# A decoder layer on one core: the score weights M stored batch by batch instead of head by head, with filler passes added at the end of TensorE's program

## The chip, the cores and the metric

The kernel runs on one core of a Trainium2 chip. The metric is the device time of one launch in microseconds (us). Every execution reads the same inputs and writes the whole output. Five queues run side by side and meet only at semaphores: PE (TensorE, the matrix engine; its weight loads are listed as PEld), DVE (VectorE), ACT (ScalarE), POOL (GpSimd) and SP (SyncE, which here issues DMAs). SBUF is the working memory that all engines read and write, PSUM the eight banks of 512 words a partition that receive TensorE's results.

## What is computed

x is (16, 256, 128): 16 batches of 256 rows; the context is (16, 64, 128). Three blocks follow one another, each with a residual and a layer norm:

```
x = layernorm(x + attn(x))     # linear attention, 16 heads of 8, elu+1 features, normalised keys
x = layernorm(x + xattn(x, context))
x = layernorm(x + ffn(x))      # fp4-quantised activations and weights, silu(gate) * up, down
# xattn, per head of 64 (16 heads, inner width 1024):
scores = einsum('bhld,bhrd->bhlr', x @ Wq, context @ Wk) * SCALE
out    = einsum('bhlr,bhrd->bhld', softmax(scores), context @ Wv) @ Wo
```

## The kernel before

The work of a batch b is done in T = 2 tiles of 128 rows. The cross attention doesn't build queries and keys. G = Wq Wk^T is made once for each head, and M = G times the transposed context gives, for each batch, a 128 x (16 heads x 64 context rows) matrix, so that the scores of a tile are one product of the transposed row tile with M. To keep the precision of fp32 with single-pass matmuls, both sides are split into a high part and a low part (type fp32r), and three products are summed (PARTS, the pairs high-high, high-low and low-high).

Sizes: HX = 16 heads, R = 64 context rows, BG = 4 batches in a group g, NG = 4 groups, and NQ = 4 quarters q of QH = 4 heads in a group. `m_product(g, q)` (L2768) makes one quarter: 12 matmuls of 256 columns (64 context rows of each of 4 batches) into a pair of PSUM banks, 1,024 words a partition, laid out head, batch, context row. `m_keep_high` (ACT, L975) copies the pair into M as the high part, `m_keep_low` (DVE, L1731) subtracts that from the bank and writes the low part. There are 16 of each over the program, eight of them before 52 us.

`scores(b, t)` (L2841) issues six matmuls of 512 columns: three products for each of two halves of the heads. The moving operand (rhs) is the slice of M of one batch; in the layout before, one head's 64 words stand 256 words from the next head's. `scores_shift` (L2855) then adds the negated row maxima: two matmuls of 512 columns whose moving operand is one word for each head, repeated 64 times.

The order of each engine's program is written out by hand as a list of calls. In PE's list, calls of 16 batches in all stages are interleaved, with `pe.wait_ge` lines between them. `keep_warm(bank, n)` (L2965) issues n matmuls of the identity with itself into a bank that nobody reads at that time. Each is a 128-column fp32 matmul, which the profile shows as two passes. Before, such fillers stand at the very start and at four places at the end of the list. The names in the last stretch: `h_transpose` and `tile_h_transpose` transpose the quantised hidden values `hv` (they wait for POOL's dequantisation, `hq_made`); `down` is the last product of the FFN; `tile_xf_transpose`, `tile_gate_up`, `tile_h_transpose` and `tile_down` do for one tile of batch 15 what the whole-batch functions do for the others; `xfT_kept` counts ACT's copies of the transposed FFN input, `hg4_made` DVE's last rounding of a batch (or tile) of hidden values, `yf_made` DVE's FFN residual. Line numbers in the rows below are those of this kernel.

Of the kernel before, what the change touches and what calls it, by code (L numbers as in the profile page):

```python
# [6 lines left out]
FP32 = mybir.dt.float32  # L7
FP32R = mybir.dt.float32r
INT32 = mybir.dt.int32
ALU = mybir.AluOpType  # L10
ACT = mybir.ActivationFunctionType
AX = mybir.AxisListType

P = 128
# [3 lines left out]
def decoder_layer(nc, x, x_t, attn_w, attn_rows, ctx_t, wq_t, wk_t, wv_t, wo_in, fw_in, out):  # L18
# [9 lines left out]
    R = ctx_t.shape[1] // B  # L28
    HA, DA = 16, 8
    HX, DX = 16, 64  # L30
# [4 lines left out]
    HC = HX // 2  # L35
    BG = 4
    NG = B // BG
    NQ = 4
    QH = HX // NQ
# [22 lines left out]
    with es:  # L62
        def sb(name, shape, dt=FP32):
            return es.enter_context(nc.sbuf_tensor(name, shape, dt))

        def banks(name, n):
            return es.enter_context(nc.psum_tensor(name, [P, n * BANK], FP32))

        def sem(name):
            return es.enter_context(nc.semaphore(name))  # L70
# [24 lines left out]
        ctx_f = sb("ctx_f", [P, B * R])  # L95
        ctx_r = sb("ctx_r", [P, 2, B * R], FP32R)
        HW = sb("HW", [P, 2, NJ, P])
        M = sb("M", [P, 2, 2, HX, BG * R], FP32R)
        w_gu = sb("w_gu", [P, 2, I])
        w_gu_r = sb("w_gu_r", [P, 2, 2, I], FP32R)  # L100
        w_dn = sb("w_dn", [P, NK, P])
# [11 lines left out]
        def several(name, n, shape, dt=FP32):  # L113
            return [sb(f"{name}{k}", shape, dt) for k in range(n)]
# [39 lines left out]
        h = several("h", 2, [P, NH, BLK + 1])  # L154
# [17 lines left out]
        A1, A2, S, TP, F = banks("A1", 1), banks("A2", 1), banks("S", 2), banks("TP", 2), banks("F", 2)  # L172
        F0, F1 = F[:, 0:BANK], F[:, BANK:2 * BANK]
        S0, S1, TP0, TP1 = S[:, 0:BANK], S[:, BANK:2 * BANK], TP[:, 0:BANK], TP[:, BANK:2 * BANK]
# [35 lines left out]
        m_made, m_high, m_low = sem("m_made"), sem("m_high"), sem("m_low")  # L210
# [18 lines left out]
        pT_made, pT_kept, o_made = sem("pT_made"), sem("pT_kept"), sem("o_made")  # L229
# [3 lines left out]
        xfT_made, xfT_kept = sem("xfT_made"), sem("xfT_kept")  # L233
# [4 lines left out]
        ht_made, hg4_made, hq_made = sem("ht_made"), sem("hg4_made"), sem("hq_made")  # L238
        hT_made, hT_kept = sem("hT_made"), sem("hT_kept")
        dn_made, yf_made = sem("dn_made"), sem("yf_made")  # L240
# [13 lines left out]
        def part(w, t):  # L254
            return w[:, t * P:t * P + P]
# [7 lines left out]
        def blocks(ap, n):  # L263
            return ap.rearrange("p (n k) -> p n k", k=BLK)
# [23 lines left out]
        M_BANKS = (TP, S, F, S, F, TP, S, F) + (TP,) * 8  # L288

        def m_bank(g, q):  # L290
            return M_BANKS[NQ * g + q][:, :].rearrange("p (h n) -> p h n", h=QH)

        def m_part(g, q, part):
            return M[:, g % 2, part, QH * q:QH * q + QH, :]

        block = es.enter_context(nc.Block())

# [658 lines left out]
        def _(act):  # L956
            sc = nc.scalar
# [17 lines left out]
            def m_keep_high(g, q):  # L975
                act.wait_ge(m_made, NQ * g + q + 1)
                if g >= 2:
                    act.wait_ge(s_made, T * BG * (g - 1))
                sc.activation(m_part(g, q, 0), m_bank(g, q), ACT.Copy).then_inc(m_high, 1)

            def hw_keep(half):
                act.wait_ge(hw_made, half + 1)
# [192 lines left out]
            k_guess_squared(1, 0)  # L1175
            k_miss_squared(1, 0)
            m_keep_high(0, 0)
            k_exp(2)
            k_guess_squared(1, 1)
            keep_v(2)  # L1180
            k_miss_squared(1, 1)
            m_keep_high(0, 1)
            attn_norm(0, 0)
            m_keep_high(0, 2)
            k_squares(2)
            attn_norm(0, 1)
# [511 lines left out]
        def _(dve):  # L1698
            ve = nc.vector
# [30 lines left out]

            def m_keep_low(g, q):  # L1731
                dve.wait_ge(m_high, NQ * g + q + 1)
                ve.tensor_tensor(m_part(g, q, 1), m_bank(g, q), m_part(g, q, 0).bitcast(FP32), ALU.subtract).then_inc(m_low, 1)

            def x1T_keep_low(b):
                dve.wait_ge(x1T_kept, b + 1)
# [1008 lines left out]
        def _(pe):  # L2745
# [95 lines left out]
            def scores(b, t):  # L2841
                g = b // BG
                pe.wait_ge(x1T_kept, b + 1)
                pe.wait_ge(x1T_low, b + 1)
                if b % BG == 0 and t == 0:
                    pe.wait_ge(m_high, NQ * g + NQ)
                    pe.wait_ge(m_low, NQ * g + NQ)
                for n, (left, right) in enumerate(PARTS):
                    for half in range(2):
                        last = te.matmul(S[:, half * BANK:half * BANK + BANK], part(x1T[b % 2][:, left, :], t),  # L2850
                                         M[:, g % 2, right, HC * half:HC * half + HC, b % BG * R:b % BG * R + R],
                                         start=(n == 0), stop=(n == len(PARTS) - 1))
                last.then_inc(s_made, 1)

# [29 lines left out]
            def xf_transpose(b):  # L2884
                pe.wait_ge(xq_made, b + 1)
                for t in range(T):
                    last = te.transpose(A2[:, t * P:t * P + P], xv[b % 2][:, t * P:t * P + P], ident[:, :])
                last.then_inc(xfT_made, 1)

            def gate_up(b, t):  # L2890
                if b == 0 and t == 0:
                    pe.wait_ge(fwT_kept, 4)
                    pe.wait_ge(gu_high_made, 2)
                    pe.wait_ge(gu_low_made, 2)
                pe.wait_ge(xfT_kept, b + 1)
                if b in WHOLE_GATE:
                    for m, bk in enumerate(ffn_banks(b)):
                        last = te.matmul(bk[:, 0:I], part(xfT[b % 2], t), w_gu[:, m, :], start=True, stop=True)
                    last.then_inc(gu_made, 1)
                    return  # L2900
                pe.wait_ge(xf_low_made, b + 1)
                for n, (left, right) in enumerate(PARTS):
                    for m, bk in enumerate(ffn_banks(b)):
                        last = te.matmul(bk[:, 0:I], part(xf_r[b % 2][:, left, :], t), w_gu_r[:, right, m, :],  # L2904
                                         start=(n == 0), stop=(n == len(PARTS) - 1))
                last.then_inc(gu_made, 1)

            def h_transpose(b):
                pe.wait_ge(hq_made, b + 1)
                for t in range(T):  # L2910
                    for k, k0 in enumerate(KC):
                        c0 = t * BANK + k * P
                        last = te.transpose(TP[:, c0:c0 + P], hv[b % 2][:, t * I + k0:t * I + k0 + P], ident[:, :])  # L2913
                last.then_inc(hT_made, 1)

            def down(b):
                pe.wait_ge(hT_kept, b + 1)
                for t in range(T):
                    if b in SUM_ON_PE:
                        pe.wait_ge(x2_made, T * b + T)  # L2920
                        te.matmul(blocks(part(DN, t), NBX), ident[:, :], x2[b % 3][:, NBX * t:NBX * t + NBX, 0:BLK],
                                  start=True, stop=False)
                    for k in range(NK):
                        last = te.matmul(part(DN, t), hT[b % 2][:, t, k * P:k * P + P], w_dn[:, k, :],  # L2924
                                         start=(k == 0 and b not in SUM_ON_PE), stop=(k == NK - 1))
                last.then_inc(dn_made, 1)
# [10 lines left out]
            def tile_xf_transpose(b, t):  # L2937
                pe.wait_ge(xq_made, b + t + 1)
                te.transpose(part(A2, t), part(xv[b % 2], t), ident[:, :]).then_inc(xfT_made, 1)

            def tile_gate_up(b, t):
                pe.wait_ge(xfT_kept, b + t + 1)
                for m, bk in enumerate(GU_OF[t]):
                    last = te.matmul(bk[:, 0:I], part(xfT[b % 2], t), w_gu[:, m, :], start=True, stop=True)
                last.then_inc(gu_made, 1)
# [19 lines left out]
            def keep_warm(bank, n, w=ident[:, :]):  # L2965

                for _ in range(n):
                    te.matmul(bank[:, 0:P], w, w, start=True, stop=True, skip_group_check=True)
# [549 lines left out]
            pe.wait_ge(yx_made, 15)  # L3518
            xf_transpose(12)
            pe.wait_ge(pT_kept, 30)  # L3520
            h_transpose(11)
            pe.wait_ge(hg4_made, 12)
            gate_up(12, 0)
# [28 lines left out]
            pe.wait_ge(h_made, 29)  # L3552
            gate_up(14, 1)
            pe.wait_ge(hT_kept, 13)
            keep_warm(TP0, 9)
            h_transpose(13)
            pe.wait_ge(yf_made, 13)
            keep_warm(A2, 4)
            tile_xf_transpose(15, 0)
            pe.wait_ge(xfT_kept, 16)  # L3560
            down(13)
            pe.wait_ge(hg4_made, 15)
            tile_gate_up(15, 0)
# [2 lines left out]
            pe.wait_ge(hg4_made, 14)  # L3566
            tile_gate_up(15, 1)
            pe.wait_ge(hT_kept, 14)
            keep_warm(TP0, 7)
            h_transpose(14)  # L3570
            pe.wait_ge(xfT_kept, 17)
            keep_warm(A2, 4)
            down(14)
# [50 lines left out]
```

## Time and profile before

| | us |
|---|---|
| median of 3 runs | 360.56 (360.54 to 360.67) |
| the profiled execution, whole | 362.69 |
| its span, first to last instruction | 360.9 |
| PE busy / DVE busy / POOL busy / ACT busy | 342.2 / 307.8 / 271.8 / 256.0 |
| mean granted TensorE clock | 0.994 |

The profiled execution is 2.1 us longer than the median of the others, and 1.8 us of it lie outside the span. A row of a stretch gives each engine's busy time and, in brackets, how many instructions it had; a row in order of time gives the start, the time from the first start to the last end, and the number of merged instructions. Matmuls are pipelined, so that the duration of one (its mean, or min/median/max) is longer than its distance to the next.

### The profile page before, as it was taken

Reading aid. Unit: us, or ns where it says so; the run is one execution under the profiler, and the core shown is the slowest. Engines: PE = TensorE matmul, PEld = TensorE weight load, DVE = VectorE, ACT = ScalarE, POOL = GpSimd, SP = SyncE. Lnnn points to the kernel's source line nnn. Section 1 sums busy time; section 2 is a strip of 40 time slices with the busy share of each in tenths; the row PEclk is TensorE's granted clock in tenths of the full one; section 3 lists DMA queues with packets and bytes.
Section 4 is the critical chain, followed back from the end, with each engine's and each line's share of the span. In section 5 each row is a group of like instructions: output and inputs, shape, how many; then the busy total and the mean of one; then the engine's idle time right before and its main releaser. Section 6 shows DMA issues by size and latency. Waiting matters only on the chain.

```text
span 360.9 us, 7621 instructions
## 1 busy us (share of the span) xinstructions
PE 342.2 (95%) x2319; PEld 288.1 (80%) x2319; DVE 307.8 (85%) x851; ACT 256.0 (71%) x533; POOL 271.8 (75%) x453
## 2 busy tenths in 40 slices
PE   6789999999999999999999999999999999989884
PEld 6588858787779979977799977888897888968763
DVE  1599986667799998988889988989999987999994
ACT  2678886776788685797857677877877767666543
POOL 3275779889978769798777578979979897794445
PEclk9899999999999999999999999999999999999999
DMA  7821100000100000111001000001000000001001
GB/s 233 290 62 31 39 8 16 0 16 2 46 29 2 1 2 0 45 32 31 0 2 40 7 1 17 15 3 29 2 1 17 1 16 15 4 15 31 0 23 37
DMA packets 13587, 10.46 MB, mean 29 GB/s; under 512 B 971, under 2 KB 12396, under 8 KB 13548
## 3 DMA queue, kind: packets, MB, share of 16 engines
q1 hardware_dynamic: 12540, 7.89, 7.2%
q10 hardware_dynamic: 1008, 2.10, 1.6%
q8 instruction: 19, 0.31, 0.4%
q14 instruction: 20, 0.16, 0.2%
HBM read 7.88 MB, written 2.10 MB: 28 GB/s over the span
## 4 chain that ended last, share of the span: by engine, by line
PE 52%; POOL 16%; issue 14%; DVE 11%; ACT 4%; DMA 1%; POOLq 0%; ACTq 0%; DVEq 0%
PE A L2880 11%; PE S L2850 8%; PE TP L2837 5%; PE TP L2868 5%; PE F L2904 4%; POOL pe L445 3%; PE A L2798 3%; PE A L2924 2%; PE S L2859 2%; POOL fold L439 2%; PE TP L2776 2%; POOL hv L455 2%; DVE smax L1838 2%; PE TP L2913 2%; DMA wqkT<-in_wk_t 1%
## 5 line engine op out<-in xcount | busy, mean ns | idle before, releaser
L445 POOL TENSOR_TENSOR pe<-pe,srec 128x1024 f32<-128x1024 f32 x32 | 60.8, 1905 | 5.0 <-DVE srec L1855 4.9
L2880 PEld LDWEIGHTS A<-wvoT,wqkT 128*128 128x128 f32 x480 | 56.1, 192 | 2.0 <-issue 1.2
L2880 PE MATMUL A<-wvoT,wqkT 128*128 128x128 f32 x480 | 57.3, 275 | 0.0
L2850 PE MATMUL S<-M,x1T 128*128 128x512 f32 x192 | 52.8, 410 | 0.7 <-DVE x1T L1737 0.7
L439 POOL TENSOR_TENSOR fold<-pe 128x512 f32<-128x512 f32 x32 | 42.1, 1314 | 12.6 <-ACT pe L1081 12.4
L2850 PEld LDWEIGHTS S<-M,x1T 128*128 128x128 f32 x192 | 34.0, 189 | 10.4 <-issue 1.8
L1838 DVE TENSOR_REDUCE smax<-S 128x16 fp32r<-128x1024 f32 x32 | 38.9, 1215 | 2.2 <-PE S L2850 2.2
L1086 ACT ACTIVATE wqkT<-TP 128x1024 f32<-128x1024 f32 x32 | 32.7, 1021 | 10.9 <-PE TP L2868 10.8
L1081 ACT ACTIVATE pe<-S 128x1024 f32<-128x1024 f32 x32 | 32.6, 1018 | 5.8 <-PE S L2859 5.6
L2868 PE MATMUL TP<-ident,pe 128*128 128x128 f32 x256 | 33.6, 274 | 0.5 <-ACT wqkT L1086 0.2
L2904 PE MATMUL F<-w_gu_r,xf_r 128*128 128x352 f32 x168 | 33.9, 337 | 0.1
L2868 PEld LDWEIGHTS TP<-ident,pe 128*128 128x128 f32 x256 | 28.8, 140 | 3.7 <-ACT wqkT L1086 0.8
L2837 PE MATMUL TP<-HW,ctx_f 128*64 128x512 f32 x128 | 31.0, 605 | 0.0
L2904 PEld LDWEIGHTS F<-w_gu_r,xf_r 128*128 128x128 f32 x168 | 27.4, 188 | 1.4 <-DVE h L1899 0.5
L1849 DVE TENSOR_REDUCE ssum<-fold 128x16 f32<-128x512 f32 x32 | 21.3, 672 | 6.1 <-POOL fold L439 6.0
L2924 PE MATMUL A<-w_dn,hT 128*128 128x128 f32 x180 | 22.9, 277 | 1.0 <-ACT xfT L1133 1.0
L430 POOL TENSOR_TENSOR kn<-fk,ky 128x256 f32<-128x256 f32 x16 | 11.1, 696 | 16.9 <-DVE ky L1803 16.7
L2924 PEld LDWEIGHTS A<-w_dn,hT 128*128 128x128 f32 x180 | 21.8, 192 | 2.3 <-ACT xfT L1133 1.2
L455 POOL TENSOR_TENSOR hv<-hv,ham 128x704 f32<-128x704 f32 x15 | 20.8, 1388 | 2.5 <-DVE hv L1925 2.4
L2859 PE MATMUL S<-smax,ident_r 128*128 128x512 f32 x64 | 21.4, 416 | 0.7 <-DVE smax L1838 0.7
L423 POOL TENSOR_TENSOR xb<-x_sb,rows 128x512 f32<-128x512 f32 x16 | 20.4, 1279 | 0.5 <-POOL x L488 0.5
L1075 ACT ACTIVATE wvoT<-TP 128x1024 f32<-128x1024 f32 x16 | 16.3, 1021 | 5.7 <-PE TP L2837 5.6
(246 smaller groups left out, 914.6 us busy)
## 6 DMA issues: line engine op xcount, KB each, us to landing
xT<-in_x_t SPq DMA_DIRECT2D x16, 128.0 KB, 2.2
x_sb<-in_x SPq DMA_DIRECT2D x16, 128.0 KB, 2.2
out<-yf SPq DMA_DIRECT2D x15, 128.0 KB, 1.8
pe<-in_fw SPq DMA_DIRECT2D x1, 560.0 KB, 10.6
wqkT<-in_wq_t ACTq DMA_DIRECT2D x2, 256.0 KB, 4.8
wqkT<-in_wk_t ACTq DMA_DIRECT2D x2, 256.0 KB, 6.3
ctx_f<-in_ctx_t ACTq DMA_DIRECT2D x2, 256.0 KB, 7.4
wvoT<-in_wv_t ACTq DMA_DIRECT2D x1, 512.0 KB, 8.9
```

Of the source, the lines that this page charges most:

```text
L439: ge.tensor_tensor(by_head(fold[n % NFO][:, :]), p4[:, :, 0, :], p4[:, :, 1, :], ALU.add).then_inc(fold_made, 1)
L445: ge.tensor_tensor(w, w, spread(srec[n % NFO][:, :], HX, R), ALU.mult).then_inc(pn_made, 1)
L1081: sc.activation(pe_[n % NPE][:, :], S[:, :], ACT.Exp, scale=SCALE).then_inc(pe_made, 1)
L1086: sc.activation(pT[n % 2], TP[:, :].rearrange("p (a n) -> p a n", a=NJ), ACT.Copy).then_inc(pT_kept, 1)
L1838: ve.tensor_reduce(smax[n % 2][:, :], by_head(S[:, :]), AX.X, ALU.max, negate=True).then_inc(smax_made, 1)
L2837: last = te.matmul(TP[par * R:par * R + R, half * BANK:half * BANK + BANK], ctx_f[:, b * R:b * R + R], HW[:, par, 4 * half:4 * half + 4, : ...
L2850: last = te.matmul(S[:, half * BANK:half * BANK + BANK], part(x1T[b % 2][:, left, :], t), M[:, g % 2, right, HC * half:HC * half + HC, b % ...
L2859: last = te.matmul(S[:, half * BANK:half * BANK + BANK], ident_r[:, :], spread(smax[n % 2][:, HC * half:HC * half + HC], HC, R), start=Fal ...
L2868: last = te.transpose(TP[:, j * P:j * P + P], pe_[n % NPE][:, j * P:j * P + P], ident[:, :])
L2880: last = te.matmul(part(A2, t), pT[n % 2][:, j, :], vo[b % 2][:, j, :], start=(j == 0 and b not in SUM_ON_PE), stop=(j == NJ - 1))
L2904: last = te.matmul(bk[:, 0:I], part(xf_r[b % 2][:, left, :], t), w_gu_r[:, right, m, :], start=(n == 0), stop=(n == len(PARTS) - 1))
L2924: last = te.matmul(part(DN, t), hT[b % 2][:, t, k * P:k * P + P], w_dn[:, k, :], start=(k == 0 and b not in SUM_ON_PE), stop=(k == NK - 1))
```

## The change

It has two parts.

1. M's axes are stored as batch, head, context row. `scores` reads 512 words in one run. The two evictions write four runs of 256 words, one for each batch, and read the bank pair as batch, head, context row, that is in 16 pieces of 64 words that stand 256 words apart within one batch. The number of words, of instructions and the order of the calls stay.
2. On PE, fillers are added: 2 ahead of `h_transpose(11)`, a fifth one to the 4 ahead of `tile_xf_transpose(15, 0)`, and 4 ahead of `down(13)`. Some waits stand twice in a row; the second is on a value already reached and merges with the first in the built program.

```
-        M = sb("M", [P, 2, 2, HX, BG * R], FP32R)
+        M = sb("M", [P, 2, 2, BG, HX, R], FP32R)
...
+        def m_by_batch(g, q):
+            return M_BANKS[NQ * g + q][:, :].rearrange("p (h b r) -> p b h r", h=QH, b=BG)
...
         def m_part(g, q, part):
-            return M[:, g % 2, part, QH * q:QH * q + QH, :]
+            return M[:, g % 2, part, :, QH * q:QH * q + QH, :]
...
-                sc.activation(m_part(g, q, 0), m_bank(g, q), ACT.Copy).then_inc(m_high, 1)
+                sc.activation(m_part(g, q, 0), m_by_batch(g, q), ACT.Copy).then_inc(m_high, 1)
...
-                ve.tensor_tensor(m_part(g, q, 1), m_bank(g, q), m_part(g, q, 0).bitcast(FP32), ALU.subtract).then_inc(m_low, 1)
+                ve.tensor_tensor(m_part(g, q, 1), m_by_batch(g, q), m_part(g, q, 0).bitcast(FP32), ALU.subtract).then_inc(m_low, 1)
...
-                                         M[:, g % 2, right, HC * half:HC * half + HC, b % BG * R:b % BG * R + R],
+                                         M[:, g % 2, right, b % BG, HC * half:HC * half + HC, :],
...
             pe.wait_ge(pT_kept, 30)
+            pe.wait_ge(pT_kept, 30)
+            keep_warm(TP0, 2)
             h_transpose(11)
...
             pe.wait_ge(hT_kept, 13)
+            pe.wait_ge(hT_kept, 13)
             keep_warm(TP0, 9)
             h_transpose(13)
             pe.wait_ge(yf_made, 13)
-            keep_warm(A2, 4)
+            pe.wait_ge(yf_made, 13)
+            keep_warm(A2, 5)
             tile_xf_transpose(15, 0)
             pe.wait_ge(xfT_kept, 16)
+            pe.wait_ge(hg4_made, 14)
+            keep_warm(S0, 4)
             down(13)
...
             pe.wait_ge(hT_kept, 14)
+            pe.wait_ge(hT_kept, 14)
             keep_warm(TP0, 7)
             h_transpose(14)
+            pe.wait_ge(xfT_kept, 17)
             pe.wait_ge(xfT_kept, 17)
             keep_warm(A2, 4)
             down(14)
```

PE ahead of `down(13)`, before (L2968 is a filler, L2939 `tile_xf_transpose(15, 0)`, L2924 `down(13)`, L2944 `tile_gate_up(15, 0)`):

```order
L2968 MATMUL A<-ident 128x128 [waits yf_made]
L2968 MATMUL A<-ident 128x128 x3
L2939 MATMUL A<-ident,xv 128x128 [waits xq_made]
L2924 MATMUL A<-w_dn,hT 128x128 [waits hT_kept,xfT_kept]
L2924 MATMUL A<-w_dn,hT 128x128 x5
L2944 MATMUL F<-w_gu,xfT 128x352 [waits xfT_kept,hg4_made]
```

The same place after (L2971 is a filler, L2942 the transpose, L2927 `down(13)`, L2947 `tile_gate_up(15, 0)`):

```order
L2971 MATMUL A<-ident 128x128 [waits yf_made]
L2971 MATMUL A<-ident 128x128 x4
L2942 MATMUL A<-ident,xv 128x128 [waits xq_made]
L2971 MATMUL S<-ident 128x128 [waits hg4_made,xfT_kept]
L2971 MATMUL S<-ident 128x128 x3
L2927 MATMUL A<-w_dn,hT 128x128 [waits hT_kept]
L2927 MATMUL A<-w_dn,hT 128x128 x5
L2947 MATMUL F<-w_gu,xfT 128x352 [waits xfT_kept,hg4_made]
```

What moved: the wait for `xfT_kept` now stands in front of the four new fillers, and `down(13)` follows them.

PE ahead of `h_transpose(11)`, before (L2887 is `xf_transpose(12)`, L2913 `h_transpose(11)`):

```order
L2887 MATMUL A<-ident,xv 128x128
L2913 MATMUL TP<-ident,hv 128x128 [waits hq_made,pT_kept]
L2913 MATMUL TP<-ident,hv 128x128 x5
```

The same place after:

```order
L2890 MATMUL A<-ident,xv 128x128
L2971 MATMUL TP<-ident 128x128 [waits pT_kept]
L2971 MATMUL TP<-ident 128x128
L2916 MATMUL TP<-ident,hv 128x128 [waits hq_made]
L2916 MATMUL TP<-ident,hv 128x128 x5
```

What moved: two fillers start as soon as `pT_kept` allows, and only the transposes behind them wait for `hq_made`.

## Rows read from the trace of the kernel before

**Rows 1.** The page: PE's busy time, and slices of the span with the granted clock

```profile
PE 342.2 (95%) x2319; PEld 288.1 (80%) x2319; DVE 307.8 (85%) x851; ACT 256.0 (71%) x533; POOL 271.8 (75%) x453
...
PEclk9899999999999999999999999999999999999999
```

**Rows 2.** Busy time by stretch: start:end length, engines, granted clock, DMA share, GB/s

```profile
20.00:30.00 10.00, 8.90 (x74) 8.28 (x73) 9.90 (x23) 7.89 (x19) 5.90 (x9) 1.00 0.14 41
...
250.00:300.00 50.00, 50.00 (x343) 41.65 (x342) 47.62 (x132) 36.01 (x71) 45.50 (x75) 1.00 0.02 7
...
340.00:350.00 10.00, 7.78 (x47) 5.79 (x47) 9.50 (x28) 4.25 (x11) 4.62 (x11) 1.00 0.01 2
```

**Rows 3.** Instructions on tile M: duration min/median/max in ns, first and last start

```profile
L2850 PE MATMUL S<-M,x1T x192: 387/394/583, 43.4 to 314.4; 128*128 128x512 f32 x192
L979 ACT ACTIVATE M<-TP x10: 1004/1024/1028, 22.6 to 197.1; 128x1024 fp32r<-128x1024 f32 x10
L1733 DVE TENSOR_TENSOR M<-TP,M x10: 1215/1224/1225, 24.8 to 198.2; 128x1024 fp32r<-128x1024 f32 x10
```

**Rows 4.** The same view of other fp32r matmuls, by their lines: L2776, L2904, L2859

```profile
L2776 PE MATMUL TP<-ctx_r,GT x120: 277/283/387, 19.4 to 196.6; 128*128 128x256 f32 x120
...
L2904 PE MATMUL F<-w_gu_r,xf_r x168: 318/324/512, 87.5 to 336.7; 128*128 128x352 f32 x168
...
L2859 PE MATMUL S<-smax,ident_r x64: 377/379/483, 46.9 to 316.6; 128*128 128x512 f32 x64
```

**Rows 5.** Groups by line and shape, DVE: busy us, mean ns, idle before

```profile
L1779 DVE SCALAR_TENSOR_TENSOR fk<-fk,A 128x256 f32<-128x256 f32 x16 | 6.6, 415 | 1.5 <-ACT vals L1012 1.3
...
L1737 DVE TENSOR_TENSOR x1T<-S,x1T 128x256 fp32r<-128x256 f32 x16 | 6.5, 407 | 0.6 <-ACT x1T L1071 0.6
```

**Rows 6.** The same view, ACT

```profile
L1071 ACT ACTIVATE x1T<-S 128x256 fp32r<-128x256 f32 x16 | 6.1, 380 | 2.0 <-PE S L2828 2.0
L1012 ACT ACTIVATE vals<-A 128x256 f32<-128x256 f32 x16 | 6.0, 377 | 0.0
```

**Rows 7.** PE in order of time around `h_transpose(11)`: start, us, instructions, idle before

```profile
317.24 0.44 PE L2887 MATMUL A<-ident,xv 128*128 128x128 f32 x2 [0.23 <-DVE yx L1860]
318.46 0.85 PE L2913 MATMUL TP<-ident,hv 128*128 128x128 f32 x6 [0.78 <-POOL hv L455]
```

**Rows 8.** PE in order of time, the last 25 us

```profile
339.92 1.06 PE L2968 MATMUL A<-ident 128*128 128x128 f32 x8
341.22 0.33 PE L2939 MATMUL A<-ident,xv 128*128 128x128 f32 x1 [0.24 <-POOL xv L517]
342.52 1.60 PE L2924 MATMUL A<-w_dn,hT 128*128 128x128 f32 x12 [0.97 <-ACT xfT L1133]
344.18 1.45 PE L2944 MATMUL F<-w_gu,xfT 128*128 128x352 f32 x4
...
351.54 1.60 PE L2924 MATMUL A<-w_dn,hT 128*128 128x128 f32 x12
352.98 0.49 PE L2951 MATMUL TP<-ident,hv 128*128 128x128 f32 x3
354.06 0.52 PE L2951 MATMUL TP<-ident,hv 128*128 128x128 f32 x3 [0.59 <-ACT hT L1145]
```

**Rows 9.** ACT in order of time, the same stretch

```profile
341.51 0.76 ACT L1106 ACTIVATE F<-hv 128x704 f32<-128x704 f32 x1 [0.58 <-DVE hv L1914]
342.21 0.26 ACT L1133 ACTIVATE xfT<-A 128x128 f32<-128x128 f32 x1
...
345.66 0.46 ACT L1137 ACTIVATE th<-F 128x352 f32<-128x352 f32 x1 [3.03 <-PE F L2944]
```

**Rows 10.** DVE in order of time, the same stretch

```profile
343.23 0.89 DVE L1925 SCALAR_TENSOR_TENSOR hv<-F,hv 128x704 f32<-128x704 f32 x1
...
344.82 0.41 DVE L1930 TENSOR_TENSOR yf<-A,x 128x256 f32<-128x256 f32 x1
...
346.18 0.50 DVE L1985 SCALAR_TENSOR_TENSOR th<-th,F 128x352 f32<-128x352 f32 x1
```

**Rows 11.** POOL in order of time, the same stretch

```profile
348.33 1.39 POOL L455 TENSOR_TENSOR hv<-hv,ham 128x704 f32<-128x704 f32 x1
...
353.13 0.78 POOL L522 TENSOR_TENSOR hv<-hv,ham 128x352 f32<-128x352 f32 x1 [0.40 <-DVE hv L2016]
```

More of the change, by code:

```diff
@@ L97, in decoder_layer @@
         HW = sb("HW", [P, 2, NJ, P])
-        M = sb("M", [P, 2, 2, HX, BG * R], FP32R)
+        M = sb("M", [P, 2, 2, BG, HX, R], FP32R)
         w_gu = sb("w_gu", [P, 2, I])
@@ L291, in m_bank, with m_by_batch @@
             return M_BANKS[NQ * g + q][:, :].rearrange("p (h n) -> p h n", h=QH)
+        def m_by_batch(g, q):
+            return M_BANKS[NQ * g + q][:, :].rearrange("p (h b r) -> p b h r", h=QH, b=BG)
         def m_part(g, q, part):
-            return M[:, g % 2, part, QH * q:QH * q + QH, :]
+            return M[:, g % 2, part, :, QH * q:QH * q + QH, :]
         block = es.enter_context(nc.Block())
@@ L978, in m_keep_high @@
                     act.wait_ge(s_made, T * BG * (g - 1))
-                sc.activation(m_part(g, q, 0), m_bank(g, q), ACT.Copy).then_inc(m_high, 1)
+                sc.activation(m_part(g, q, 0), m_by_batch(g, q), ACT.Copy).then_inc(m_high, 1)
             def hw_keep(half):
@@ L1732, in m_keep_low @@
                 dve.wait_ge(m_high, NQ * g + q + 1)
-                ve.tensor_tensor(m_part(g, q, 1), m_bank(g, q), m_part(g, q, 0).bitcast(FP32), ALU.subtract).then_inc(m_low, 1)
+                ve.tensor_tensor(m_part(g, q, 1), m_by_batch(g, q), m_part(g, q, 0).bitcast(FP32), ALU.subtract).then_inc(m_low, 1)
             def x1T_keep_low(b):
@@ L2850, in scores @@
                         last = te.matmul(S[:, half * BANK:half * BANK + BANK], part(x1T[b % 2][:, left, :], t),
-                                         M[:, g % 2, right, HC * half:HC * half + HC, b % BG * R:b % BG * R + R],
+                                         M[:, g % 2, right, b % BG, HC * half:HC * half + HC, :],
                                          start=(n == 0), stop=(n == len(PARTS) - 1))
@@ L3520, in _ @@
             pe.wait_ge(pT_kept, 30)
+            pe.wait_ge(pT_kept, 30)
+            keep_warm(TP0, 2)
             h_transpose(11)
@@ L3554, in _ @@
             pe.wait_ge(hT_kept, 13)
+            pe.wait_ge(hT_kept, 13)
             keep_warm(TP0, 9)
@@ L3557, in _ @@
             pe.wait_ge(yf_made, 13)
-            keep_warm(A2, 4)
+            pe.wait_ge(yf_made, 13)
+            keep_warm(A2, 5)
             tile_xf_transpose(15, 0)
             pe.wait_ge(xfT_kept, 16)
+            pe.wait_ge(hg4_made, 14)
+            keep_warm(S0, 4)
             down(13)
@@ L3568, in _ @@
             pe.wait_ge(hT_kept, 14)
+            pe.wait_ge(hT_kept, 14)
             keep_warm(TP0, 7)
             h_transpose(14)
+            pe.wait_ge(xfT_kept, 17)
             pe.wait_ge(xfT_kept, 17)
```

## The prediction

> **What bounds the kernel now.** I read the page first: PE is busy 95% of the span, more than any other engine, and its granted clock is full in all but one early slice [rows 1]. The stretches say where that holds: from 250 to 300 us PE is busy 50.00 of 50 us, and in the last part it isn't, with 7.78 of 10 us from 340 to 350, while DVE has 9.50 of these [rows 2]. So there are two regimes. Up to about 315 us a shorter matmul shortens the program; in the last 25 us the time is set by a chain that goes from PE to ACT, DVE and POOL and back for the last tile, and there the question is which wait ends last. The first half of the change (M's layout) touches the first regime, the second half (fillers) the last.
>
> **The scores passes.** All 192 of them change their read from eight runs of 64 words to one run of 512. What would they gain? The trace has fp32r matmuls that already read one run: 283 ns at 256 columns and 324 ns at 352 (medians), beside 394 ns for the scores at 512 [rows 3, 4]. The first two give (324 - 283) / 96 = 0.427 ns a column; carried on to 512 columns that is 324 + 160 x 0.427 = 392.3 ns. The pieced read stands 1.7 ns above the line of the unbroken ones. By this the change is worth 192 x 1.7 ns = 0.3 us, and as the extrapolation is no better than a few ns I enter 0. The other end is the scores' shift, also 512 columns and eight pieces, but of one repeated word each: 379 ns, 15 ns less [rows 4]. If one long run were read as easily as a repeated word, the gain would be 192 x 15 ns = 2.9 us, nearly all of it in PE's full stretch. Below zero there is no reason: a run has no jump that the pieces lacked. I take 0, since the contiguous rows are of the kind that the new read will be, and keep 0 to -2.9 us.
>
> The Trainium skill, SBUF — State Buffer, has a note on cachelines (in the section Door 1: The DMA port swizzle) that an access which crosses to a new 16-byte line pays and that repeated hits on a line don't; Advanced Engine Details and Errata, PSUM Cachelines, goes further with "Any non-contiguous AP significantly slows down matmuls". By the first the old and the new read cross the same number of lines, since a piece is 64 whole words, and nothing changes; by the second, taken for the moving operand, the old scores are the slow ones and the second rival below happens. The rows at 256, 352 and 512 columns speak for the first.
>
> **The evictions.** 16 on ACT (median 1,024 ns) and 16 on DVE (1,224 ns) [rows 3] keep their 1,024 words but take them in pieces. Nothing in the trace reads a bank pair in 64-word pieces. The nearest rows read 128-word pieces that stand 256 words apart: on DVE 415 ns against 407 ns for 256 words in one run [rows 5], on ACT 377 ns against 380 ns [rows 6]. On DVE that is 8 ns for two pieces at most; if it were 4 ns a piece, 16 pieces would be 64 ns an eviction, 0.5 us for the eight up to 52 us, where DVE is nearly full (9.90 of 10 us from 20 to 30 [rows 2]), and under cover of other work for the rest. The other end is ACT's -3 ns, nothing. I take 0: ACT's row shows none, and DVE's two lines are different operations. Bounds 0 to +0.5 us.
>
> **Two fillers ahead of h_transpose(11).** A filler is two passes; eight passes took 1.06 us with the last one's 0.275 us tail, so one follows the other after (1.06 - 0.275) / 7 = 0.112 us [rows 8]. The two transposes ahead end at 317.24 + 0.44 = 317.68, and PE then idles 0.78 us until POOL's hidden values let it go at 318.46 [rows 7]. Four passes put right behind them take 4 x 0.112 = 0.45 us and would leave PE free by 318.13, 0.3 us ahead of that. Cost 0, covered by the wait for POOL; without that cover 0.45 us.
>
> **The fifth filler.** Four fillers start at 339.92; ten passes instead of eight leave PE free at 341.04. The transpose behind starts at 341.22, when POOL is done [rows 8]. Cost 0. Should it slip, ACT's copy of that transpose doesn't start before 342.21 because it stands behind an earlier 0.76 us activation [rows 9], so there are 0.66 us more of cover (342.21 less 341.22 + 0.33).
>
> **Four fillers ahead of down(13).** Here the place matters. PE idles 0.97 us before `down(13)`, until 342.52, for ACT's copy [rows 8], which ends at 342.21 + 0.26 = 342.47 [rows 9]. But the wait for that copy stands before the fillers, as the order after shows. They can't fill the idle time; they start when it ends. So `down(13)` starts at 342.52 + 8 x 0.112 = 343.42, 0.90 us late. What is next:
> - `tile_gate_up(15, 0)` started at 344.18, although `down(13)` would have let it start at 342.52 + 12 x 0.112 = 343.86. It was waiting for DVE's rounding, over at 343.23 + 0.89 = 344.12 [rows 8, 10]. These 0.32 us absorb a part: it now starts at 343.42 + 1.34 = 344.76, 0.58 late.
> - ACT's tanh on it ran at 345.66 to 346.12 and DVE's product at 346.18 [rows 9, 10]. DVE goes from there without a pause to the last tile's values, so the 0.58 us go on to POOL's last dequantisation, 353.13 to 353.91 [rows 11], which becomes 354.49.
> - `down(13)`'s residual on DVE moves from 344.82 to 345.08 at the earliest, 0.25 late [rows 10]. Through POOL's order this delays the dequantisation at 348.33 [rows 11] and then `down(14)` at 351.54 [rows 8] by the same 0.25. Less than 0.58, so it doesn't set the end.
> - The last tile's transposes start at 354.06 [rows 8]. Two things released them, POOL at 353.91 and ACT's copy of the tile before at about 354.00; the second only moves by some 0.4. So they start at 354.49 + 0.06 = 354.55, 0.49 late, and everything behind them follows.
>
> The end moves by +0.5 us; that is the one term of the sum that isn't zero. Its bounds are 0.2 us (should the copy chain absorb more) and the full 0.9 us.
>
> **What fillers could give.** They give time only where the granted clock would fall without them. In the stretches I read the clock is 1.00 at 250 to 300 and still 1.00 at 340 to 350, where PE is idle a fifth of the time [rows 2], and no slice after the second is below the others [rows 1]. There is nothing to win back.
>
> **The sum.** 0 + 0 + 0 + 0.5. The profiled execution would go from 362.69 to 363.2 us, its span from 360.9 to 361.4, and the median, 2.1 us below the profiled one, from 360.56 to 361.1 us (+0.14%). A measurement of this kernel can tell about 0.2%, 0.72 us, from no change: below 359.84 is faster, above 361.28 slower.
>
> **The rivals.**
> - *The forecast*, 361.1 us: passes unchanged, tail +0.5.
> - *The run pays, in part*: the extra at 512 columns is partly the jumps. With 5 ns a pass, 192 x 5 = 1.0 us less and the tail added: 360.1. With two thirds of the 15 ns it would be 359.1. For: 394 ns lies above the line, even if little. Against: only 1.7 ns.
> - *The run pays in full*: -2.9 + 0.5 gives 358.2. For: the 379 ns of the shift [rows 4]. Against: the unbroken reads at 256 and 352 columns, which would then have to lie lower by as much.
> - *Slower*: the four fillers ahead of `down(13)` cost their full price. This needs DVE's rounding (344.12) to end 0.3 us earlier or not to matter, so that the slack before `tile_gate_up(15, 0)` is gone: +0.9, 361.5. The slack of 0.32 us decides. With the eviction's upper bound added, 362.0. For: the order puts them behind the wait. Against: the slack is in the trace.
> - *It doesn't do what it says*: the read may not be cheaper because a matmul's pattern of eight 64-word pieces is already no cost. That is the forecast without its tail, 360.6, if the fillers hide after all.
>
> **How the numbers follow.** The forecast and the case without its tail have 0.55 together (0.42 and 0.13); the run pays in part 0.15, in full 0.10; slower 0.20. Of the forecast's own spread of some 0.3 us a fifth lies above 361.28, which adds 0.08 to slower. Faster by over 0.2%: the full case and about two thirds of the partial one, 0.20. Slower: 0.28. Within: 0.52. The range leaves out the full case and the eviction's upper end: 359.1 to 361.8.
>
> **What would show it.** Right: the scores' median stays at 390 to 396 ns, the evictions at about 1,020 and 1,220 ns; PE's row of `down(13)` starts 0.9 us after its ACT copy ends, with eight passes of the identity between, and the time from there to the end of the span stays about the same but for 0.3 to 0.4 us. Wrong: a scores median near 379 ns, or a PE busy time smaller by 1 us or more in spite of 14 more passes (seven fillers); an eviction over 1,070 (ACT) or 1,280 ns (DVE); a granted clock below 1.00 in the last 40 us of either kernel.

## The result and the profile after

| | before | after |
|---|---|---|
| median of 12 runs each, us | 360.71 (360.54 to 361.31) | 361.52 (361.02 to 362.0) |
| ratio of the times | | 1.002, 95% interval 1.0011 to 1.0029 |
| profiled execution, us | 362.69 | 361.64 |
| its span, us | 360.9 | 359.8 |
| PE busy, us | 342.2 | 343.9 |

The changed kernel is slower by 0.2%, which is 0.7 us (0.4 to 1.0; the two medians themselves differ by 0.81); the forecast was +0.5. The spans say the opposite, 359.8 against 360.9, and that has to be cleared up first. Inputs landed at different times in the two profiled executions. ACT's first work that waits for data, the copy of the context, in order of time, of before:

```profile
8.37 0.63 ACT L968 ACTIVATE ctx_r<-ctx_f 128x512 fp32r<-128x512 f32 x1 [2.27 <-DMA ctx_f<-in_ctx_t]
```

and of after:

```profile
7.24 0.63 ACT L971 ACTIVATE ctx_r<-ctx_f 128x512 fp32r<-128x512 f32 x1 [1.04 <-DMA ctx_f<-in_ctx_t]
```

The change touches neither these loads nor anything ahead of them. After starts 1.1 us earlier there, and from about 20 us until the last 20 the two traces run 1.6 to 1.7 us apart. So a position in one trace is compared with the other only as a distance from a near event. I take the start of `tile_xf_transpose(15, 0)`, the transpose behind the fillers on bank A, at 341.22 us in before [rows 8] and at 339.55 us in after, and call it the mark.

The instructions on tile M, after (duration min/median/max in ns, first and last start), which answer to [rows 3]:

```profile
L2853 PE MATMUL S<-M,x1T x192: 387/394/586, 41.7 to 312.7; 128*128 128x512 f32 x192
L982 ACT ACTIVATE M<-TP x10: 1005/1024/1030, 20.8 to 195.5; 128x1024 fp32r<-128x1024 f32 x10
L1736 DVE TENSOR_TENSOR M<-TP,M x10: 1215/1225/1225, 23.2 to 196.6; 128x1024 fp32r<-128x1024 f32 x10
```

The scores pass takes 394 ns as before, the evictions 1,024 and 1,225 ns against 1,024 and 1,224. These are the ten evictions from the banks TP; the other six on ACT have medians of 1,019 and 1,026 ns here against 1,007 and 1,010 before, but 1,008 and 1,009 with the layout alone (below), so that these few ns aren't the layout's. The layout changed no duration that the traces can tell.

PE in order of time, after, where the first three rows answer to [rows 7] and the others to [rows 8]:

```profile
315.59 0.44 PE L2890 MATMUL A<-ident,xv 128*128 128x128 f32 x2 [0.23 <-DVE yx L1863]
315.87 0.61 PE L2971 MATMUL TP<-ident 128*128 128x128 f32 x4
316.73 0.87 PE L2916 MATMUL TP<-ident,hv 128*128 128x128 f32 x6 [0.25 <-POOL hv L458]
...
338.24 1.28 PE L2971 MATMUL A<-ident 128*128 128x128 f32 x10
339.55 0.33 PE L2942 MATMUL A<-ident,xv 128*128 128x128 f32 x1
340.84 1.16 PE L2971 MATMUL S<-ident 128*128 128x128 f32 x8 [0.97 <-ACT xfT L1136]
341.84 1.50 PE L2927 MATMUL A<-w_dn,hT 128*128 128x128 f32 x12
343.18 1.35 PE L2947 MATMUL F<-w_gu,xfT 128*128 128x352 f32 x4
...
350.12 1.60 PE L2927 MATMUL A<-w_dn,hT 128*128 128x128 f32 x12
351.79 0.52 PE L2954 MATMUL TP<-ident,hv 128*128 128x128 f32 x3
352.97 0.52 PE L2954 MATMUL TP<-ident,hv 128*128 128x128 f32 x3 [0.66 <-ACT hT L1148]
353.32 1.74 PE L2964 MATMUL A<-w_dn,hT 128*128 128x128 f32 x12
```

The reader is to see three things. The idle 0.97 us for ACT's copy is still there, word for word, but it now stands ahead of the fillers, and eight passes of the identity follow it. The other two groups of added fillers lie in waits: behind the two ahead of `h_transpose(11)` PE is still idle 0.25 us, and behind the ten passes on bank A the transpose starts 1.31 us after the first of them, as it did behind eight (341.22 - 339.92 = 1.30, [rows 8]). Both groups stand ahead of the mark, so what they cost would show in the distance from `xf_transpose(12)`, just ahead of the first of them, to the mark: 339.55 - 315.59 = 23.96 us, against 341.22 - 317.24 = 23.98 us before [rows 7, 8]. And the program ends later counted from the mark: the last product ends at 353.32 + 1.74 = 355.06, 15.51 us behind it, against 354.42 + 1.74 = 356.16, 14.94 us behind it, in the kernel before. That is the +0.57 us.

### The profile page after: what moved, and what is told of

The parts are those of the page before. It is cut to its first block, busy times and chain, and to the rows that moved or that the text cites. A ratio compares the mean times of both kernels' runs of the same rounds, so it can differ in the third digit from the quotient of the medians.

```text
span 359.8 us, 7653 instructions
## 1 busy us (share of the span) xinstructions
PE 343.9 (96%) x2333; PEld 290.6 (81%) x2333; DVE 307.7 (86%) x851; ACT 256.2 (71%) x533; POOL 272.2 (76%) x453
## 3 DMA queue, kind: packets, MB, share of 16 engines
q10 hardware_dynamic: 1008, 2.10, 1.6%
## 4 chain that ended last, share of the span: by engine, by line
PE 69%; DVE 15%; issue 6%; ACT 6%; POOL 4%; POOLq 0%; DVEq 0%; ACTq 0%
PE A L2883 14%; PE S L2853 10%; PE TP L2840 7%; PE TP L2871 6%; PE F L2907 6%; PE A L2927 3%; PE S L2862 3%; PE A L2801 2%; PE TP L2779 2%; PE TP L2916 2%; PE A L2809 2%; DVE smax L1841 2%; PE A L2825 2%; PE A L2971 2%; PE A L2814 1%
## 5 line engine op out<-in xcount | busy, mean ns | idle before, releaser
L1084 ACT ACTIVATE pe<-S 128x1024 f32<-128x1024 f32 x32 | 32.6, 1019 | 5.8 <-PE S L2862 5.6
L2927 PE MATMUL A<-w_dn,hT 128*128 128x128 f32 x180 | 22.8, 276 | 0.1
L2927 PEld LDWEIGHTS A<-w_dn,hT 128*128 128x128 f32 x180 | 21.8, 192 | 1.1 <-issue 0.6
```

The source lines that it names most:

```text
L1084: sc.activation(pe_[n % NPE][:, :], S[:, :], ACT.Exp, scale=SCALE).then_inc(pe_made, 1)
```

## Experiments: one part at a time

Theory: the layout costs and gives nothing, and the whole step is the four fillers behind the wait for `xfT_kept`. Rivals: the layout costs by itself (a wide interval could hide that), or each added pass costs.

**Layout alone.** The changed kernel with the fillers of before:

```
-            keep_warm(TP0, 2)
             h_transpose(11)
...
-            keep_warm(A2, 5)
+            keep_warm(A2, 4)
...
-            pe.wait_ge(hg4_made, 14)
-            keep_warm(S0, 4)
             down(13)
```

> M stored batch by batch, fillers at the end as before the change. Theory (the layout is free, the fillers cost): 360.7 us, within 0.1 us of the kernel before; scores pass median 394 ns, evictions 1,024 and 1,225 ns. Rival (the layout itself costs, through the evictions in 64-word pieces or through the passes): 0.3 to 0.8 us above the kernel before.

Measured: 360.8 us, ratio 1.0 (0.9991 to 1.0009). From the mark to the end it has the 14.94 us of before: PE in order of time,

```profile
338.95 0.33 PE L2942 MATMUL A<-ident,xv 128*128 128x128 f32 x1 [0.24 <-POOL xv L520]
340.25 1.60 PE L2927 MATMUL A<-w_dn,hT 128*128 128x128 f32 x12 [0.97 <-ACT xfT L1136]
...
352.14 1.75 PE L2964 MATMUL A<-w_dn,hT 128*128 128x128 f32 x12
```

352.14 + 1.75 - 338.95 = 14.94. The median of the pass was 396 ns; it was 395 ns in the next run, which has the layout of before, so 1 or 2 ns are no difference. The layout is free, to within 0.3 us.

**Fillers alone.** The kernel before with the seven added fillers.

```
             pe.wait_ge(pT_kept, 30)
+            keep_warm(TP0, 2)
             h_transpose(11)
...
-            keep_warm(A2, 4)
+            keep_warm(A2, 5)
             tile_xf_transpose(15, 0)
             pe.wait_ge(xfT_kept, 16)
+            pe.wait_ge(hg4_made, 14)
+            keep_warm(S0, 4)
             down(13)
```

> M as before the change, with the seven added fillers. Theory: the whole step, +0.6 us on the kernel before (361.3), and PE's down(13) starts 0.9 us after the ACT copy that it waits for. Rival (the layout costs): +0.2 us or less.

Measured: 361.53 us, ratio 1.0017 (1.0008 to 1.0026), that is +0.6 us (0.3 to 0.9), the whole step within the intervals. PE starts at 340.26 with the fillers and at 341.25 with `down(13)`, 0.99 us later, where 0.90 was expected. From the mark (338.96) to the end (352.74 + 1.74 = 354.48) it is 15.52 us, as with the whole change.

**Without the four on bank S.** The changed kernel, the other three fillers kept.

```
-            pe.wait_ge(hg4_made, 14)
-            keep_warm(S0, 4)
             down(13)
```

> The changed kernel without the four fillers ahead of down(13); the two ahead of h_transpose(11) and the fifth one ahead of tile_xf_transpose(15, 0) stay. Theory: these three are covered, so the time is that of the kernel before, 360.7. Rival (each added filler costs its 0.22 us): 361.3.

Measured: 361.02 us, ratio 1.0007 (0.9998 to 1.0016), which by itself could be 0.0 or 0.5 us. Its trace decides. PE in order of time:

```profile
315.19 0.44 PE L2890 MATMUL A<-ident,xv 128*128 128x128 f32 x2 [0.23 <-DVE yx L1863]
...
339.11 0.33 PE L2942 MATMUL A<-ident,xv 128*128 128x128 f32 x1
...
352.31 1.74 PE L2964 MATMUL A<-w_dn,hT 128*128 128x128 f32 x12
```

The three fillers stand between the first two rows, which are 339.11 - 315.19 = 23.92 us apart, against 23.98 us in the kernel before. From the mark to the end (352.31 + 1.74 = 354.05) it is 14.94 us again. The three are covered, and the whole loss is the four fillers'.

**The same four, ahead of the wait.** As many passes as in the changed kernel, one line moved.

```
             tile_xf_transpose(15, 0)
-            pe.wait_ge(xfT_kept, 16)
             pe.wait_ge(hg4_made, 14)
             keep_warm(S0, 4)
+            pe.wait_ge(xfT_kept, 16)
             down(13)
```

> The changed kernel with the same four fillers ahead of the wait for xfT_kept instead of behind it, so that they run in PE's idle 0.97 us. Theory (the place of the wait decides, not the number of passes): 360.7, as the kernel before, with as many passes as the changed one. Rival (it is the number of passes, or of waiting groups): 361.3.

Measured: 360.74 us, ratio 0.9999 (0.9991 to 1.0008). PE in order of time shows them in the former idle time, and `down(13)` 1.29 us behind the mark, as in the kernel before (1.30):

```profile
339.62 0.33 PE L2942 MATMUL A<-ident,xv 128*128 128x128 f32 x1
339.78 1.06 PE L2971 MATMUL S<-ident 128*128 128x128 f32 x8
340.91 1.60 PE L2927 MATMUL A<-w_dn,hT 128*128 128x128 f32 x12
...
352.82 1.74 PE L2964 MATMUL A<-w_dn,hT 128*128 128x128 f32 x12
```

From the mark to the end it is 352.82 + 1.74 - 339.62 = 14.94 us. It is the place and not the number. (The eight passes take 0.90 us and the idle time was 0.97 us, so that they just fit; with more of them there this run says nothing.)

**Eight instead of four, behind the wait.** `keep_warm(S0, 8)`.

> The changed kernel with eight fillers instead of four behind the wait for xfT_kept, ahead of down(13). Theory (each filler there is on the chain, two passes of 0.112 us, with the 0.3 us of slack already used up by the first four): 0.9 us above the changed kernel, 362.3 to 362.4, +1.5 on the kernel before. Rival (the step comes from there being a waiting group, not from its length): as the changed kernel, 361.5.

Measured: 362.4 us, ratio 1.0041 (1.0028 to 1.0053), that is +1.5 us on the kernel before. PE in order of time:

```profile
339.41 0.33 PE L2942 MATMUL A<-ident,xv 128*128 128x128 f32 x1
340.71 2.05 PE L2971 MATMUL S<-ident 128*128 128x128 f32 x16 [0.97 <-ACT xfT L1136]
342.60 1.50 PE L2927 MATMUL A<-w_dn,hT 128*128 128x128 f32 x12
...
354.08 1.74 PE L2964 MATMUL A<-w_dn,hT 128*128 128x128 f32 x12
```

From the mark to the end 16.41 us. The first four cost 15.51 - 14.94 = 0.57, the next four 16.41 - 15.51 = 0.90, which is 8 x 0.112. Put the other way, `down(13)` starts 0.99 us late with four and 342.60 - 339.41 - 1.30 = 1.89 us late with eight, the end comes 0.57 and 1.47 us late, and 0.42 us are absorbed both times. So the slack of the place (0.3 us of it was read off the rows of before) is used up once.

## Experiments: do the fillers that were there do anything?

The prediction said that with a granted clock of 1.00 there is nothing to win back, and added nothing on the fillers that the kernel already has. This run takes those away.

```
-            keep_warm(TP0, 9)
             h_transpose(13)
             pe.wait_ge(yf_made, 13)
-            keep_warm(A2, 4)
             tile_xf_transpose(15, 0)
...
-            keep_warm(TP0, 7)
             h_transpose(14)
             pe.wait_ge(xfT_kept, 17)
-            keep_warm(A2, 4)
             down(14)
```

> The kernel before without any filler in its last 25 us (24 fillers fewer; the 13 at the start stay). Theory (no filler gives anything back where the granted clock is full anyway): 360.7 or up to 0.2 us less, granted clock 1.00 to 357 us. Rival (the fillers keep the clock up): the granted clock falls to half in the idle stretches behind 337 us and the time rises by 0.5 us or more.

Measured: 363.01 us, ratio 1.0067 (1.0047 to 1.0087). My theory was wrong for these fillers and the rival, which asked for 0.5 us or more, was right. Busy time by stretch (start:end length, PE, PEld, DVE, ACT, POOL, granted clock, DMA share, GB/s):

```profile
334.00:338.00 4.00, 2.57 (x18) 2.09 (x17) 3.93 (x11) 1.82 (x4) 2.31 (x7) 1.00 0.00 0
338.00:340.00 2.00, 1.13 (x6) 0.86 (x6) 2.00 (x7) 0.73 (x2) 0.87 (x2) 0.80 0.00 0
340.00:342.00 2.00, 0.55 (x2) 0.18 (x1) 1.88 (x7) 1.73 (x4) 0.40 (x1) 0.50 0.00 0
342.00:344.00 2.00, 1.91 (x9) 1.91 (x10) 1.97 (x4) 0.21 (x2) 0.00 (x0) 0.50 0.00 0
344.00:346.00 2.00, 2.00 (x8) 1.50 (x8) 1.31 (x8) 0.00 (x0) 0.60 (x3) 0.50 0.00 0
346.00:352.00 6.00, 3.14 (x14) 1.66 (x12) 4.95 (x14) 3.60 (x9) 3.61 (x8) 1.00 0.08 23
352.00:354.00 2.00, 1.75 (x11) 1.78 (x12) 1.86 (x5) 0.58 (x2) 0.78 (x1) 0.71 0.22 66
354.00:358.00 4.00, 3.66 (x21) 2.93 (x20) 2.25 (x10) 1.59 (x4) 2.07 (x6) 0.72 0.00 0
```

and PE in order of time:

```profile
338.87 1.23 PE L2913 MATMUL TP<-ident,hv 128*128 128x128 f32 x6 [2.25 <-POOL hv L455]
340.88 0.45 PE L2939 MATMUL A<-ident,xv 128*128 128x128 f32 x1 [0.78 <-POOL xv L517]
342.09 2.93 PE L2924 MATMUL A<-w_dn,hT 128*128 128x128 f32 x12 [0.76 <-ACT xfT L1133]
...
350.11 0.85 PE L2913 MATMUL TP<-ident,hv 128*128 128x128 f32 x6 [1.11 <-POOL hv L455]
352.25 2.37 PE L2924 MATMUL A<-w_dn,hT 128*128 128x128 f32 x12 [1.29 <-ACT hT L1110]
...
355.94 1.73 PE L2961 MATMUL A<-w_dn,hT 128*128 128x128 f32 x12
```

PE was idle for 2.25 us ahead of 338.87, and the granted clock went from 1.00 to 0.50, the lower of its two levels (1.2 instead of 2.4 GHz). The mean of 0.80 over 338 to 340 us puts the fall at about 339.2, so the 0.78 us of idle time ahead of 340.88 came after it and isn't its cause. `down(13)` takes 2.93 us in place of 1.60 [rows 8]. The clock is full again from 346 to 352 us and then falls a second time: PE was idle 1.11 us ahead of 350.11 and 1.29 us ahead of 352.25, `down(14)` takes 2.37 us in place of 1.60 [rows 8], and the means of 0.71 and 0.72 put this fall at about 352.8 to 356.2. With the fillers of before, the longest idle time from 334 us on is the 0.97 us ahead of `down(13)` [rows 8] and the clock stays at 1.00.

From the mark (340.88) to the end (357.67) it is 16.79 us, 1.85 more than in the kernel before. Of these, 1.47 us are there when `tile_gate_up(15, 1)` starts (347.57, 6.69 us behind the mark against 5.22), which is the first fall, and 1.48 us when POOL starts its last dequantisation (354.27, 13.39 us against 11.91). The other 0.37 us are added behind that, where the clock is at 0.50 again. The mean granted clock of the other five runs was 0.980 to 0.989, against 0.993 to 0.999 in those of the kernel before beside them, so the falls aren't peculiar to the profiled execution. So the fillers of before are worth about 2 us. Which of the four groups is needed wasn't tested. The seven of the change are worth nothing, since the kernels without them (layout alone, the kernel before) already keep the full clock until PE's last product has ended.

## Experiments: when does the layout of a moving operand count?

The layout did nothing. Is that because no layout does, or because 64 words are a long piece? First M was stored as head, context row, batch, so that a pass reads and an eviction writes single words 4 apart. The evictions read the bank in 64-word pieces, as in the changed kernel.

```
-        M = sb("M", [P, 2, 2, HX, BG * R], FP32R)
+        M = sb("M", [P, 2, 2, HX, R, BG], FP32R)
...
-            return M[:, g % 2, part, QH * q:QH * q + QH, :]
+            return M[:, g % 2, part, QH * q:QH * q + QH, :, :].rearrange("p h r b -> p b h r")
...
-                                         M[:, g % 2, right, HC * half:HC * half + HC, b % BG * R:b % BG * R + R],
+                                         M[:, g % 2, right, HC * half:HC * half + HC, :, b % BG],
```

> M stored as head, context row, batch, so that a scores pass reads 512 single words that stand 4 words apart, and the evictions write single words 4 apart; fillers as before the change. Theory (a piece boundary costs nothing as long as the pieces are long, single words are another case): the scores median rises above 394 ns, or stays, in which case the layout of this read doesn't matter at all; if it rises by the share of words in a line, to twice, PE gets 192 x 0.2 us = 40 us more and the time is about 395 us. Rival (no layout of the moving words matters): 394 ns and 360.8 us. Evictions: 1,024 and 1,225 ns by both.

Measured: 422.01 us, ratio 1.1694 (1.1672 to 1.1715). Instructions on tile M:

```profile
L2853 PE MATMUL S<-M,x1T x192: 623/660/807, 48.9 to 373.3; 128*128 128x512 f32 x192
L982 ACT ACTIVATE M<-TP x10: 2010/2057/2112, 21.1 to 235.3; 128x1024 fp32r<-128x1024 f32 x10
L1736 DVE TENSOR_TENSOR M<-TP,M x10: 1993/2036/2060, 24.3 to 237.4; 128x1024 fp32r<-128x1024 f32 x10
```

The pass went from 394 to 660 ns. The evictions, for which I had expected no change, doubled on ACT and rose by two thirds on DVE; they write, and DVE also reads back, words that stand 4 apart. So that theory fell for the evictions, and the time came out above the 395 us that it gave. To have the read by itself, four more kernels keep the stores of before and change the pattern of the read alone, with K = 1, 2, 4 and 16 (the pass then reads words of all four batches, which changes the values and not the work):

```
-                                         M[:, g % 2, right, HC * half:HC * half + HC, b % BG * R:b % BG * R + R],
+                                         M[:, g % 2, right, HC * half:HC * half + HC, :].rearrange("p h (x c k) -> p (h x) c k", c=BG, k=K)[:, :, b % BG, :],
```

> The kernel before, evictions and fillers untouched; only a scores pass reads its 512 words of M in pieces of 1 word that stand 4 apart (it then reads words of all four batches of the group, so that the scores aren't the reference's; the number of words, instructions and orders is). Theory (what cost time with single words was the read itself): a median of about 660 ns for the pass, as with the words stored 4 apart, and evictions at 1,024 and 1,225 ns again. Rival (the read is cheap and the pass was slowed by the bank or by the evictions beside it): 394 ns.

> The same with pieces of 2 words that stand 8 apart; again words of all four batches. Theory (the price is per piece boundary, hidden if the next piece is asked for early enough): 394 ns already, or half the extra of single words, 527 ns. Rival (any gap costs, only few gaps cost little): per gap 266 ns / 512 = 0.52 ns, that is 394 + 256 x 0.52 = 527 ns.

> The same with pieces of 4 words that stand 16 apart; words of all four batches. Theory: 394 ns, a piece fills a whole 16-byte line. Rival (0.52 ns a gap): 394 + 128 x 0.52 = 460 ns.

> The same with pieces of 16 words that stand 64 apart; words of all four batches. Theory: 394 ns. Rival (0.52 ns a gap): 394 + 32 x 0.52 = 411 ns, which a median can tell apart.

The pass on tile M and ACT's eviction, K = 1:

```profile
L2850 PE MATMUL S<-M,x1T x192: 622/660/808, 41.6 to 355.2; 128*128 128x512 f32 x192
L979 ACT ACTIVATE M<-TP x10: 1004/1024/1029, 20.6 to 218.8; 128x1024 fp32r<-128x1024 f32 x10
```

K = 2:

```profile
L2850 PE MATMUL S<-M,x1T x192: 622/658/809, 41.5 to 355.1; 128*128 128x512 f32 x192
```

K = 4:

```profile
L2850 PE MATMUL S<-M,x1T x192: 380/403/593, 41.9 to 313.1; 128*128 128x512 f32 x192
```

K = 16:

```profile
L2850 PE MATMUL S<-M,x1T x192: 382/407/596, 41.2 to 313.5; 128*128 128x512 f32 x192
```

| piece, words | pass, median ns | time, us (one run; before 360.32) |
|---|---|---|
| 1 | 660 | 403.78 |
| 2 | 658 | 403.68 |
| 4 | 403 | 361.41 |
| 16 | 407 | 361.84 |
| 64 (before) | 394 | 360.32 |
| 512 (after) | 394 | |

Single words are slow because of the read itself, since the evictions are back at 1,024 ns there. The rival's price of 0.52 ns a gap is refuted: 4 words would give 460 ns, and 2 words 527. My theory for 2 words (394 or 527 ns) was wrong too. It is a step: nothing but a few ns from 4 words on, and the full price at 1 and 2. What the four runs don't separate is the length of a piece from the distance between pieces, which grew with it (4, 8, 16 and 64 words), and pieces of 3 words weren't run.

The duration of a pass understates the price, because passes overlap. Six of them in a row, in the kernel before:

```profile
313.16 1.64 PE L2850 MATMUL S<-M,x1T 128*128 128x512 f32 x6
```

and with K = 1:

```profile
352.83 3.01 PE L2850 MATMUL S<-M,x1T 128*128 128x512 f32 x6
```

Without the duration of the last one that is (1.64 - 0.39) / 5 = 0.25 us from one start to the next before and (3.01 - 0.66) / 5 = 0.47 with single words: nearly twice, and not two thirds more. Over 192 passes 0.22 us are 42 us, and the run took 43.5 us longer. The kernel with the words stored 4 apart took 422.01 us, some 18 us more than K = 1 with the same 660 ns for a pass; that part goes with its slower evictions. The Trainium skill (SBUF — State Buffer, Door 1: The DMA port swizzle) says that SBUF has 16-byte lines and that at least two hits a line are needed for full bandwidth. Four words are 16 bytes, and the trace agrees that a whole line is enough (403 ns, if M starts on a line, which the traces don't show); it doesn't agree on two hits, as pieces of 2 words took 658 ns. The 9 to 13 ns of K = 4 and 16 above 394 ns are small and not ordered by the number of gaps; what they are stays open. So does their price: these kernels ran once each, 1.1 and 1.5 us above the single run of before beside them, and the runs of before in this document already lie 1.1 us apart (360.3 to 361.4). ACT's eviction doubles through its write, as its read of the bank is that of the changed kernel, where it took 1,024 ns; for DVE the runs don't tell the write from the second read, that of the high part.

## Why the prediction came out as it did, point by point

- **The passes: right, and shown.** The forecast entered 0, from the line through the unbroken reads at 256 and 352 columns (392.3 ns expected, 394 measured before, 394 after). The full and the partial gain are excluded by the layout alone (ratio 1.0). The shift's 379 ns [rows 4], which carried those rivals, is no price of an ordinary contiguous read: one unbroken run of 512 words takes 394.
- **The cachelines: weighed rightly.** A run of 64 words doesn't pay, a single word does. The Trainium skill's sentence that any non-contiguous pattern slows matmuls stands under PSUM Cachelines (Advanced Engine Details and Errata), and the prediction stretched it to a moving operand in SBUF. There, of the pieces tried, only those of 1 and 2 words pay clearly (660 and 658 ns); what pieces in PSUM do to a matmul no run here shows.
- **The evictions: right.** 0 entered, 0 to +1 ns found on the banks TP, with a bank pair read in 64-word pieces. The upper bound of 0.5 us wasn't needed.
- **Two fillers, and the fifth: right.** Both covered: from `xf_transpose(12)` to the mark it is 23.92 us in the run without the four and 23.96 in the changed kernel, 23.98 before.
- **The four ahead of down(13): right in place and mechanism.** Counted from the mark, before and after in us:

| step | before | after | moved | forecast |
|---|---|---|---|---|
| `down(13)` starts | 1.30 | 2.29 | 0.99 | 0.90 |
| `tile_gate_up(15, 0)` starts | 2.96 | 3.63 | 0.67 | 0.58 |
| ACT's tanh starts | 4.44 | 5.01 | 0.57 | 0.58 |
| DVE's product starts | 4.96 | 5.51 | 0.55 | 0.58 |
| dequantisation of batch 14 starts | 7.11 | 7.36 | 0.25 | 0.25 |
| last dequantisation starts | 11.91 | 12.49 | 0.58 | 0.58 |
| last tile's last transposes start | 12.84 | 13.42 | 0.58 | 0.49 |

The starts of ACT, DVE and POOL after are these rows, each in its engine's order of time. ACT:

```profile
344.56 0.46 ACT L1140 ACTIVATE th<-F 128x352 f32<-128x352 f32 x1 [3.60 <-PE F L2947]
```

DVE:

```profile
345.06 0.52 DVE L1988 SCALAR_TENSOR_TENSOR th<-th,F 128x352 f32<-128x352 f32 x1 [0.23 <-ACT th L1140]
```

POOL:

```profile
346.91 1.39 POOL L458 TENSOR_TENSOR hv<-hv,ham 128x704 f32<-128x704 f32 x1
...
352.04 0.79 POOL L525 TENSOR_TENSOR hv<-hv,ham 128x352 f32<-128x352 f32 x1 [0.40 <-DVE hv L2019]
```

Two terms were mis-sized, both are small, and only the second reaches the end. `down(13)` came 1.00 us behind the first filler and not 0.90: the first step between two groups took about 0.1 us more than the 0.112 us of a pass. `tile_gate_up` started 0.67 late, but its four passes took 1.35 instead of 1.45 us, so that ACT saw 0.57 where 0.58 was forecast. And at the very end I took 0.06 us from POOL's release to the transposes, which is the distance to ACT's copy of before (354.00 to 354.06). After, POOL's dequantisation ends at 352.83 and the transposes start at 352.97, 0.14 us, and before it was 0.15 as well (353.91 to 354.06). This turns the 0.49 that I summed into the 0.57 found. ACT's copy, for which I had said some 0.4 us, moved by 0.50 (353.51 and 352.34, each counted from its mark) and ended at 352.83 too, so that which of the two released PE there can't be told.
- **The sum and the runs.** +0.57 us from the traces, +0.72 us (0.40 to 1.05) from the times. The interval holds the former; whether 0.1 us more comes from elsewhere can't be told.
- **The slower rival** had +0.9 us from the missing slack. The slack was there, as the eight fillers show (0.57, then 0.90).
- **What fillers could give: half right.** For the seven added ones the clock was full without them, and they gave nothing. I hadn't considered that the clock was full because of the fillers that stand there. One of my signs of being wrong, a granted clock below 1.00 in the last 40 us, did appear in both kernels (means of 0.85 before and 0.67 after from 356 us on). PE had only 0.16 us of work left there before and none after, so the sign came without a cost; it should have been limited to the time in which PE still has work.
- **The span that was forecast (361.4) was wrong.** It was 359.8, because the start of the profiled execution of before had been late: its 362.69 us were 2.1 us above the median. I had seen that difference and carried it into the forecast of the profiled time; the distance to the median is a property of that execution and not of the kernel.

## What to carry to other kernels

A filler behind a wait delays its engine by its full length, the same filler ahead of it is free as long as it fits into the idle time (here 0.90 us of passes in 0.97): look in the built order where the wait stands, and put fillers between the last useful instruction and the wait that they are to bridge. A delay that is put on one engine arrives at the end reduced by the slack of the next waits, once; the second helping costs in full. Before fillers are judged useless because the clock is full, take away those that stand there already. In this kernel a moving operand of fp32 words in pieces of 64 cost nothing against one run, and pieces of 4 and 16 words at most about 1.5 us over 192 passes; single and double words nearly doubled the time that each pass holds PE.

## What the runs showed of the hardware that I had not expected

- Pieces of 1 and of 2 words cost the same (660 and 658 ns for 512 columns), pieces of 4 words 403 ns. The distances between the pieces were 4, 8 and 16 words.
- ACT's eviction with writes 4 words apart took 2,057 ns for 1,024 words against 1,024 ns, DVE's subtraction 2,036 against 1,224 ns.
- Without the end's fillers, the granted clock fell to 0.50 twice: from about 339.2 to 346 us, behind 2.25 us of idle time on PE, and from about 352.8 to 356.2 us, behind idle times of 1.11 and 1.29 us. With idle times of at most 1 us there the clock stayed at 1.00. The two falls together cost the kernel 2 us.
